# First layer of a four-layer kernel: TensorE's second product of a tile uses the register that the first product loaded

## The reference, cut to what matters

```python
def _L0_xattn_ref(hidden_states, token_ids, Wg, Wu, Wd):   # E = 4 experts, all three weights are ctx_2048
    expert_ids = jnp.minimum(tid // tokens_per_expert, E - 1)
    for e in range(E):
        g = jax.nn.silu(jnp.einsum('bsd,fd->bsf', hidden_states, Wg[e]))
        u = jnp.einsum('bsd,fd->bsf', hidden_states, Wu[e])
        y = jnp.einsum('bsf,df->bsd', g * u, Wd[e])
        out = jnp.where((expert_ids == e)[..., None], y, out)
...
x = x + jnp.tanh(g_xattn[0]) * _L0_xattn_ref(_layernorm(x, axis=-1), itok_BxS_13_99985, ctx_2048, ctx_2048, ctx_2048)
```

## Time and profile before

| | us |
|---|---|
| median of 3 runs | 1135.02 (1132.65 to 1138.77) |
| the profiled execution, its own time | 1131.66 |
| its span in the trace | 1129.8 |
| TensorE busy in the span | 988.2 (87%) |
| DVE / ACT / POOL busy | 696.2 / 677.3 / 516.4 |
| first layer's tiles on TensorE, first `up` to last `down` | 41.5 to 220.8 |

### The profile page before, as it was taken

How to read it: one execution, slowest core, us unless ns; L and a number is a source line. 1 busy time by engine, 2 the same in 40 slices (tenths; PEclk the granted TensorE clock), 3 DMA queues, 4 the chain that set the end, 5 groups by cost and what they waited for, 6 DMA issues and landing times.

```text
span 1129.8 us, 27372 instructions
## 1 busy us (share of the span) xinstructions
PE 988.2 (87%) x9516; PEld 571.6 (51%) x9516; DVE 696.2 (62%) x1645; ACT 677.3 (60%) x1100; POOL 516.4 (46%) x446
## 2 busy tenths in 40 slices
PE   5889999888999989999999999975799999988840
PEld 2555555556667667777777777742122222212220
DVE  7676764558879744334444332216487788876687
ACT  4555654544445346556566554444788898999940
POOL 0322332137767456666567555532222454454323
PEclk9999999998999999999999999997899999999965
DMA  7534232257889188888888777776668977787311
GB/s 242 181 128 136 95 117 74 113 147 129 185 211 212 42 286 168 188 180 182 213 202 178 152 132 121 138 119 168 148 140 166 199 156 163 165 186 129 67 44 66
DMA packets 184819, 171.35 MB, mean 152 GB/s; under 512 B 137444, under 2 KB 140068, under 8 KB 183780
## 3 DMA queue, kind: packets, MB, share of 16 engines
q1 hardware_dynamic: 157650, 112.33, 39.7%
q0 software_dynamic: 25888, 56.43, 24.8%
q10 hardware_dynamic: 1154, 0.87, 0.2%
HBM read 80.87 MB, written 65.20 MB: 129 GB/s over the span
## 4 chain that ended last, share of the span: by engine, by line
PE 53%; DVE 15%; DMA 14%; issue 8%; ACT 5%; POOL 4%; SPq 1%; ACTq 0%; DVEq 0%; POOLq 0%
PE ps_shpY L1523 10%; PE ps_shpH L1534 10%; PE ps_shpH L402 6%; PE ps_atpO L1872 5%; PE ps_shpY L845 4%; PE ps_shpH L835 4%; PE ps_atpS L1862 4%; ACT sb_atp L2111 3%; PE ps_atpP L1895 3%; DMA x2a<-sb_roy,sb_roentry 3%; DMA sb_ropiece<-rw 2%; DMA sb_quxT<-sb_quxhl 2%; DMA sb_roxg<-xn,sb_roentry 2%; DVE sb_shxs L1317 1%; DMA sb_shxT<-sb_shxhl 1%
## 5 line engine op out<-in xcount | busy, mean ns | idle before, releaser
L2111 ACT ACTIVATE sb_atp<-ps_atpS 128x1024 f32<-128x1024 f32 x256 | 247.7, 1025 | 27.4 <-PE ps_atpS L1862 26.7
L1534 PEld LDWEIGHTS ps_shpH<-sb_roxT,sb_rowt 128*128 (+1 forms) x2844 | 167.2, 106 | 18.8 <-issue 0.4
L1534 PE MATMUL ps_shpH<-sb_roxT,sb_rowt 128*128 128x128 f16 (+1 forms) x2844 | 171.8, 219 | 0.1
L1523 PE MATMUL ps_shpY<-sb_rowt,sb_rohhl 128*128 (+1 forms) x711 | 166.5, 379 | 5.1 <-DVE sb_rohhl L1397 5.1
L1872 PE MATMUL ps_atpO<-sb_atp,sb_atv 128*17 128x512 f32 x1024 | 135.9, 603 | 0.1
L1235 ACT ACTIVATE sb_roh<-ps_shpH,sb_rob 128x128 f32<-128x128 f32 (+1 forms) x237 | 68.9, 361 | 79.2 <-PE ps_shpH L1534 71.7
L1132 POOL DMA_INDIRECT sb_roxg<-xn,sb_roentry x79 | 86.4, 1094 | 53.9 <-issue 28.6
L1862 PE MATMUL ps_atpS<-sb_atq,sb_atk 64*128 64x512 f16 x512 | 97.1, 391 | 15.0 <-ACT sb_atp L2111 12.4
L1862 PEld LDWEIGHTS ps_atpS<-sb_atq,sb_atk 64*128 64x128 f16 x512 | 24.4, 93 | 158.1 <-ACT sb_atp L2111 88.6
L1523 PEld LDWEIGHTS ps_shpY<-sb_rowt,sb_rohhl 128*128 128x128 f16 (+1 forms) x711 | 66.4, 98 | 71.5 <-issue 6.4
L1224 ACT ACTIVATE sb_roy<-ps_shpY,sb_roentry 128x512 f32<-128x512 f32 x79 | 54.1, 685 | 68.7 <-PE ps_shpY L1523 45.1
(11 more groups left out here) (362 smaller groups left out, 1751.0 us busy)
## 6 DMA issues: line engine op xcount, KB each, us to landing
sb_rowt<-rw SPq DMA_DIRECT2D x15, 768.0 KB, 8.4
sb_rowt<-rw SPq DMA_DIRECT2D x15, 704.0 KB, 5.7
kst<-sb_kykp SPq DMA_DIRECT2D x16, 512.0 KB, 2.9
qst<-sb_quqp SPq DMA_DIRECT2D x12, 512.0 KB, 3.6
vst<-sb_kyvt SPq DMA_DIRECT2D x16, 272.0 KB, 2.4
sb_atv<-vst SPq DMA_DIRECT2D x32, 136.0 KB, 3.6
sb_stage<-ctxT SPq DMA_DIRECT2D x4, 1024.0 KB, 5.8
sb_shxin<-x SPq DMA_DIRECT2D x16, 256.0 KB, 6.4
```

Source lines behind the costliest of these rows:

```text
L1523: last = e.matmul(pY[it.p][:, :], hhl[it.p][0:n, x, k * P:(k + 1) * P], weight(value, 2 * W1 + w + k * D, n, D), start=j == 0, stop=j == l ...
L1534: last = e.matmul(rpH[it.p][0:n, f * P:(f + 1) * P], weight(ex["up"], w + k * FF + f * P, P, n), rxT[it.p][:, x + k, :], start=j % (3 * KD ...
L2111: S.done(e.activation(pr[n % 6][:, :], pS[n % 2][:, :], ACT.Exp, scale=HD ** -0.5 / SA ** 2), "atexp")
```

## The change

In `tensor`, `up(n)` keeps the register with the expert's number of tile n in a dictionary, and `down(n)`, which runs a beat later, takes it from there. The second `value_load` of the same number is gone; the waits, the products and their order stay.

```diff
         W = KD * D
         ch, cl = self.part["ctx"]
+        expert = {}
...
         def up(n):
-            ex = e.value_load(K["tab1"][0:1, n:n + 1], min_val=0, max_val=min(n, E1 - 1))
+            ex = expert[n] = e.value_load(K["tab1"][0:1, n:n + 1], min_val=0, max_val=min(n, E1 - 1))
             e.wait_ge(S.sem("sulo"), 3 + min(n, E1 - 1) if n else 2)
...
         def down(n):
-            ex = e.value_load(K["tab1"][0:1, n:n + 1], min_val=0, max_val=min(n, E1 - 1))
+            ex = expert[n]
             S.wait(e, "l1hl", turn_of(n))
             S.wait(e, "l1y", turn_of(n - 1))
```

## The result

The changed kernel took 1121.42 us (median of 4 runs, 1119.74 to 1125.75); the kernel before, measured beside it on the same chip, took 1133.84 us. The ratio is 0.9891 with a 95% interval of [0.9852, 0.993]: faster by 12.4 us, where 11.4 were forecast. In the changed kernel the lines behind the edit stand one lower: the first product is L836, the second L846, the load L829.

A forecast was written before the change was run, and what follows sets the result against it. The prediction took TensorE's order in the first layer, idle before second products, as the bound. Gains of 11.0 + 0.2 + 0.6 - 0.4 = 11.4 us from the median 1135.02 gave 1123.6 us, range 1119.5 to 1128.8.

The forecast's parts named there:

- What bounds the layer: First layer: TensorE's own order is the path, with 0.71 us idle per 9.35 us beat, ahead of the second product.
- The load and its followers: Ahead of the second products of tiles 2 to 15: removing load, register operation and assert saves 11.0 us.
- Tile 1: Second product of tile 1: the load lies in TensorE's 3.6 us wait for DVE, so 0 is gained.
- Tiles 16 to 18: Last tiles of the first layer: ACT and DVE work limits the gain to 0.2 us, at tile 16.
- The address operations: Second product: its address operations go, 0.10 us per tile on the path, +0.6 us over six tiles.
- the second may find all four ready: With one register for both products, the second product's four addresses per tile need no recomputing; bounded by 0 and 1.4 us.
- DVE's new waits: Second products near tiles 7 and 9: TensorE newly waits 0.15 and 0.3 us for DVE's L743, giving back 0.4 us.
- The address operations stay: Rival, second product: its address operations remain and nothing else changes; gain 10.8 us, 1124.2 us; chance 0.25.
- DVE takes the place: Rival, first layer: DVE or ACT limits the faster beat; gain about 9.5 or 7.0 us, the latter 1128.0 us; chance 0.12.
- Hidden already: Rival, second product: the load is already hidden, or a later stage absorbs the gain; 1135.0 us; chance 0.09 together.
- Slower by saved registers: Rival, first product: keeping numbers and addresses adds register operations; sixteen per tile would give 1155 us; chance 0.03.

The follow-up runs named there:

- e3_load_twice: The kernel before with a second load of the same number ahead of the second product, the first value unused: 1142.92 us, ratio 1.0103.
- e10_before: The kernel before, unchanged, run once more for a second trace: 1123.84 us in its one run.
- e1_after: The changed kernel run again, unchanged, with more rounds: 1120.58 us, ratio 0.9908 to the kernel before.
- e11_after_again: The changed kernel run a third time, unchanged: 1120.64 us, ratio 0.9896 to the kernel before.
- e2_both_early: The kernel before with both loads of the expert's number in the first product, in two registers, none in the second: 1120.08 us, ratio 0.9905.
- e9_filler: The changed kernel with 56 unread matmuls where TensorE waits for DVE ahead of tile 1's second product: 1121.06 us, ratio 0.9935 to the kernel before.
- e7_number_early: The changed kernel with a tile's one load moved ahead of the key projection of the beat before: 1125.67 us, ratio 0.9913 to the kernel before.
- e5_after_between: The changed kernel with the key projections moved between first and second product: 1124.67 us, ratio 0.9887 to the kernel before.
- e6_after_two_in_up: The changed kernel with a second, unused load of the same number in the first product: 1128.96 us, ratio 0.9918 to the kernel before.
- e4_keys_between: The kernel before, its load in place, with the key projections moved between first and second product: 1122.36 us, ratio 0.9921.

## Why the prediction was right

**What bounds the layer**: right. TensorE's order was the path, the idle pieces at the second product were the load's, and they fell when the load fell, doubled when it was doubled and vanished when it was covered.

**The load and its followers, 11.0**: right. 14 tiles with a mean gap of 1.02 before and 0.23 after are 11.05 us, in which the two small terms below are contained. `e3_load_twice` gives some 0.65 for one load, where the prediction had 0.64 from 0.47 of instructions and the hand-overs.

**Tile 1, 0**: nothing was gained there, as forecast, but two details were wrong. The wait there did not grow by the 0.6 that the prediction named (3.6 before, 3.4 after; 3.4 too in `e10_before`). The step confused two waits: only the sequencer's wait grows by the load's time; TensorE's idle stretch runs from the end of the first product to DVE's release, and the load moves neither. The stretch at the lower clock did not spread to the key, for which the prediction held 2.59 us in reserve: the key behind it took 2.69 us (68.92 to 71.61) against 2.59. It did take the second product whole: 5.07 us from its start to the key in the changed kernel, 4.28 before. The other traces vary as much (3.89 in `e10_before`, 5.07 and 3.96 in `e1_after` and `e11_after_again`; the key of `e1_after` took 2.90), so it isn't put down to the edit.

**Tiles 16 to 18, 0.2**: right. From tile 16's second product to the last one it is 10.46 and 10.25 us before, 10.78, 10.82 and 10.83 after: some 0.45 of tile 16's 0.66 is lost again behind ACT and DVE, as the earlier trace rows had it. One thing behind it was overlooked. TensorE's wait ahead of the last second product, 1.07 us in both traces of before, is 2.24, 2.28 and 2.29 in the three of the changed kernel, and in the latter two the granted clock was 0.50 and 0.57 in 206 to 209 us: that product took 4.1 and 4.0 us up to the next key instead of 2.6.

**The address operations, +0.6**: wrong, the mis-sized term. The step that failed is "the second may find all four ready": the product of number and width is reused, but an addition stays (FUSED_REGOPS became ALU_OP, 144 of them). `e2_both_early`, which has the old operations, has the same gap within 0.01 us. So the term is about 0.1 us for the layer, where the prediction had 0.6, from 0.10 a tile on the path.

**DVE's new waits, -0.4**: too large, and worked out from two shifts that were both off. Where a second product waits for L743 in `e9_filler`, it starts 0.24 us behind the end of L743. In the three traces of the changed kernel that is seen at tile 9, with 0.09 us in one and 0.12 in another (forecast 0.3), and at tile 7 in one, with 0.24 (forecast 0.15); the mean of the three is 0.15. At tile 7 of the changed kernel DVE ends L743 at 116.96 + 0.74 = 117.70 and the sequencer comes to its wait at 117.8, so 0.1 us is to spare:

```profile
116.96 0.74 DVE L743 SCALAR_TENSOR_TENSOR sb_l1y<-ps_shpY,sb_gate,sb_l1x 128x512 f32<-128x512 f32 x1
```

```profile
L119 PEldq EVENT_SEMAPHORE  x1: 51/51/51, 117.8 to 117.8; - x1
```

(DVE in order of time, and TensorE's sequencer.) Of the 1.73 us by which L743 is earlier than in the earlier trace rows, 1.2 lie ahead of tile 1. Counted from tile 1's second product, DVE moved ahead by 0.55 us and not by 1.2, and TensorE asks 0.8 us later than forecast (53.95 against 118.15 - 65.03 = 53.12), as long as the slower clock at tile 1 had held it (5.07 against 4.28). Of the two misses the second is the larger, and hides the first. In `e11_after_again`, where that product took 3.96, the wait at tile 7 is there.

The two errors, +0.5 and -0.25, nearly cancel, which is luck: 11.05 in the gaps, with both terms in it, and 0.2 behind tile 16 are 11.25, against 11.0 measured over the stretch and 10.4 to 12.4 in the timed comparisons.

**What was to be seen after**: the beat is 8.62 (forecast 8.6 to 8.8), the last second product starts at 206.39 (forecast 206.6; without the 1.2 us ahead of tile 1 it would be 207.6), the waits of the second product on "issue" are gone (forecast under 1 us), and the first product has its 16 address operations a tile as before.

**The rivals.** "The address operations stay" was true in its mechanism, and its 10.8 us is nearer to the stretch than the forecast's 11.4; the timed ratios don't separate them. "DVE takes the place" didn't happen, but `e9_filler` shows how near it was: 1.4 to 1.9 us more of speed in the first beats and it does. "Hidden already" is excluded by `e3_load_twice`. The prediction cited the Trainium skill (TensorE: Matmul & The Clock Gate, section Architectural detail) for a queue of 64 instructions, by which both loads would have cost nothing. What the runs show is that the sequencer does lead TensorE, by 2.4 us at 164.0 in `e7_number_early`, and that this lead is spent on the first product's operations; a queue's depth says only how long the lead can be. "Slower by saved registers" did not show: no operation was added.

**What stays open.** From the last second product's start to the end of the span it took 911.8 and 904.4 us before, and 917.5, 921.6 and 913.7 in the three traces of the changed kernel. One of the prediction's signs of being wrong, a last second product 11 us earlier without an end that is, half showed in the first trace: the span is 5.9 us shorter (1123.9 against 1129.8) with that product 11.65 us earlier. But the profiled executions are single ones. Those of the changed kernel took 4.3, 8.9 and 0.15 us more than the medians of their comparisons, and those of before 3.4 and 4.3 less than theirs; if these differences lie behind the layer, as most of the kernel does, the distances become 915.2 and 908.7 before, and 913.2, 912.7 and 913.6 after. A part of the layer's gain could still be given back there, by a few us at most; the slower last second product of two traces, 1.4 to 1.5 us, is such a part. Most of the spread lies in the stage of the shared experts of the second layer, where TensorE waits for transposes made by DMA: over all thirteen traces the whole distance varies by 18.5 us, and the one to the end of this line's matmuls by 12.6. The waits of that line, one row each from the kernel before:

```profile
PE ps_shpR L1437 <- DMA sb_shxT<-sb_shxhl: 12.5, 5, 4.5
```

from `e10_before`:

```profile
PE ps_shpR L1437 <- DMA sb_shxT<-sb_shxhl: 8.8, 3, 6.0
```

and from the changed kernel and `e5_after_between`:

```profile
PE ps_shpR L1438 <- DMA sb_shxT<-sb_shxhl: 8.4, 4, 5.6
```

```profile
PE ps_shpR L1438 <- DMA sb_shxT<-sb_shxhl: 17.2, 6, 6.9
```

The traces `e1_after` and `e11_after_again` have 13.5 and 8.2. They scatter from 8.2 to 17.2 us, in the changed kernel alone from 8.2 to 13.5, and don't follow the length of the distance either (8.4 with 917.5, 12.5 with 911.8), so they are not all of it. The timed comparisons, 12.4, 10.4 and 11.8 us, speak for the layer's 11 us reaching the end whole; their intervals are some 4 us either way. No kernel here beat the changed one by more than its interval.

## What to carry to other kernels

A register load from on-chip memory costs TensorE its whole sequencer time, here 0.65 us, where it stands right behind a run of short matmuls whose addresses are computed one by one; a second one behind a key of 512-column matmuls costs a quarter to a third of that (0.15 and 0.23), and a single one nothing that these runs could tell. So look in the trace at how far the sequencer is ahead at each place, load there where the lead is long, and reuse the register. Before counting on a faster beat, look which engine is next, here DVE with 0.1 us to spare at tile 7.

## What the runs showed of the hardware

- A second covered load isn't free: `e6_after_two_in_up` paid 0.15 us a tile for it, inside the product behind it. I read the sequencer's lead as a stock that this product draws on; `e2_both_early`, with the longer address form as well, paid 0.23.
- The lead has an upper end. At 164.0 us in `e7_number_early`, when the first product's address operations began to come at TensorE's own pace, 9 key matmuls and 8 transposes were still to start: 34 instructions with their weight loads, and 40 with the three matmuls and weight loads that the first pair of operations serves. The weight loads of that stretch (163.9 to 166.5 us):

```profile
163.84 1.82 PEld L402 LDWEIGHTS ps_shpH<-sb_wk,sb_ctx 128*128 128x128 f16 x9
165.78 0.65 PEld L303 LDWEIGHTS ps_shpY<-sb_ident,sb_l1xhl 128*128 128x128 f16 x8
```

  The Trainium skill (TensorE: Matmul & The Clock Gate, section Architectural detail) has 64 for the depth of TensorE's queue. If that pace means a full queue, which no run here shows apart, this trace has it full at 34 to 40.
- In the changed kernel the granted clock was at its lower level of 1.2 GHz (0.50 in 65 to 68 us) after TensorE's wait of 3.4 us at tile 1, and that product took 5.07 us against 2.58 in `e9_filler` (64.32 to 66.90). In `e11_after_again`, with a wait of 3.3 us, it was 0.75 there. It held 1.00 where the key filled that wait (`e4_keys_between`: 0.8 us left of it; `e5_after_between`: 0.6). Between these the length of the wait alone doesn't decide: with 2.7 us in either, `e2_both_early` kept the clock and `e6_after_two_in_up` didn't:

```profile
65.00:68.00 3.00, 3.00 (x16) 1.34 (x14) 2.74 (x7) 1.45 (x2) 2.19 (x3) 1.00 0.75 279
```

```profile
65.00:68.00 3.00, 3.00 (x9) 1.06 (x8) 2.83 (x7) 1.36 (x2) 2.11 (x3) 0.54 0.80 286
```

- A shorter wait can cost the clock too. In `e3_load_twice` it was 1.00 up to 157 us and 0.57 in 157 to 161, behind an idle piece of 1.92 us, and the second product there took 4.28 us instead of 2.6. An idle piece of 1.91 us two tiles later, in the same trace, left the clock at 1.00 (179 to 185 us).
